# Gated cross-attention block: the next head group's scores ahead of this group's value products, and a second place for the exponentials

## The reference

```python
x = x + tanh(g_xattn[0]) * attention(layernorm(x), ctx, Wq, Wk, Wv, Wo)
# scores = Q K^T / sqrt(32); attn = softmax(scores) over 154 keys; out = (attn V) Wo^T
x = x + tanh(g_ffn[0]) * ffn(layernorm(x), W_r, W_k, W_v, mu_r, mu_k)
# x_prev = x shifted by one token
# xr = mu_r x + (1 - mu_r) x_prev, xk likewise with mu_k
# out = sigmoid(xr W_r^T) * (square(relu(xk W_k^T)) W_v^T)
```

## Time and profile before

| | |
|---|---|
| median of 3 runs | 1349.93 us |
| the profiled execution, whole | 1352.5 us |
| its span, first to last instruction | 1350.8 us |
| mean granted TensorE clock | 0.997 |
| TensorE busy with matmuls | 1324.2 us, 98% |
| TensorE weight loads | 992.8 us, 73% |
| VectorE | 1046.6 us, 77% |
| ScalarE | 778.0 us, 58% |
| GpSimd | 659.6 us, 49% |

### The profile page before, as it was taken

The page is one execution under the profiler, slowest core; times in us unless marked ns, Lnnn a source line. Parts: engine busy times, 40 slices in busy tenths (PEclk is TensorE's granted clock), DMA queues, the critical chain, the costliest instruction groups (busy, mean ns, idle before and its releaser), DMA issues.

```text
span 1350.8 us, 28900 instructions
## 1 busy us (share of the span) xinstructions
PE 1324.2 (98%) x9776; PEld 992.8 (73%) x9776; DVE 1046.6 (77%) x1983; ACT 778.0 (58%) x1457; POOL 659.6 (49%) x843
## 2 busy tenths in 40 slices
PE   6999999999999999999999999999999999999998
PEld 5667687777768677776877768777776877768777
DVE  6878778787886878778787887878788687877763
ACT  7655737466474655737466473745737465573633
POOL 7524445454444545445454445545445554444434
PEclk9998999999999999999999999999999999999999
DMA  9521312424123242312424222242413324231011
GB/s 311 155 59 48 91 51 78 116 55 128 44 84 77 62 132 54 99 45 77 112 54 132 59 77 66 62 132 54 122 33 85 93 54 139 54 92 48 32 48 40
DMA packets 160732, 113.27 MB, mean 84 GB/s; under 512 B 107456, under 2 KB 122304, under 8 KB 160704
## 3 DMA queue, kind: packets, MB, share of 16 engines
q1 hardware_dynamic: 160704, 112.91, 29.3%
HBM read 72.43 MB, written 35.39 MB: 80 GB/s over the span
## 4 chain that ended last, share of the span: by engine, by line
PE 88%; DVE 8%; ACT 3%; issue 1%; DMA 0%; DVEq 0%; ACTq 0%
PE g_bank L1415 41%; PE g_bank L1606 10%; PE o_bank L1546 7%; PE g_bank L1502 6%; PE s_bank L1520 4%; PE d_bank L1552 4%; PE s_bank L1530 3%; PE s_bank L1415 3%; PE s_bank L1478 3%; DVE buf L1006 2%; DVE o_bank L1194 2%; PE o_bank L1421 1%; DVE d_bank L1194 1%; PE s_bank L1524 1%; PE d_bank L1421 1%
## 5 line engine op out<-in xcount | busy, mean ns | idle before, releaser
L1099 DVE TENSOR_TENSOR pq<-s_bank,pq 128x512 f16<-128x512 f32 x320 | 220.0, 688 | 73.4 <-ACT s_bank L798 72.1
L1095 DVE TENSOR_REDUCE mm<-s_bank 128x3 f32<-128x462 f32 (+1 forms) x384 | 198.8, 578 | 74.6 <-PE s_bank L1478 74.6
L797 ACT ACTIVATE pq<-s_bank 128x512 f16<-128x512 f32 x320 | 194.3, 607 | 101.2 <-PE s_bank L1524 101.2
L798 ACT ACTIVATE s_bank<-s_bank 128x512 f32<-128x512 f32 x320 | 197.0, 616 | 0.0
L1606 PE MATMUL g_bank<-buf,WkT 128*128 128x512 f32 x720 | 189.7, 409 | 3.4 <-DVE buf L1006 3.3
L1415 PE MATMUL g_bank<-WrT,buf 128*128 128x512 f32 x744 | 183.7, 396 | 0.0
L1415 PE MATMUL g_bank<-WoT,buf 128*128 128x512 f32 (+1 forms) x768 | 175.4, 374 | 0.0
L1415 PE MATMUL g_bank<-WvT,buf 128*128 128x512 f32 x708 | 174.3, 395 | 0.0
L1415 PEld LDWEIGHTS g_bank<-WrT,buf 128*128 128x128 f32 x744 | 137.2, 188 | 39.3 <-issue 10.8
L1606 PEld LDWEIGHTS g_bank<-buf,WkT 128*128 128x128 f32 x720 | 131.4, 191 | 43.9 <-DVE buf L1006 9.6
L1415 PEld LDWEIGHTS g_bank<-WvT,buf 128*128 128x128 f32 x708 | 130.7, 188 | 32.4 <-issue 5.4
(11 more groups left out here) (186 smaller groups left out, 2304.6 us busy)
## 6 DMA issues: line engine op xcount, KB each, us to landing
xa<-in_x SPq DMA_DIRECT2D x64, 256.0 KB, 4.2
x<-in_x SPq DMA_DIRECT2D x64, 256.0 KB, 2.8
xt_scratch<-xa SPq DMA_DIRECT2D x28, 512.0 KB, 3.1
xnT_loaded<-xt_scratch SPq DMA_DIRECT2D x112, 128.0 KB, 3.2
out<-x SPq DMA_DIRECT2D x48, 256.0 KB, 2.3
place<-x SPq DMA_DIRECT2D x16, 256.0 KB, 2.4
out<-place SPq DMA_DIRECT2D x16, 256.0 KB, 2.0
k_all<-k_scratch SPq DMA_DIRECT2D x15, 256.0 KB, 3.3
```

Source lines behind the costliest of these rows:

```text
L797: nc.scalar.activation(pq[:, n, HI, :], bank[:, :], ACT.Exp, scale=SCALE).then_inc(p_hi, 1)
L798: nc.scalar.activation(bank[:, :], bank[:, :], ACT.Exp, scale=SCALE).then_inc(p_full, 1)
L1095: nc.vector.reduce_max(maxima, scores, AX.X).then_inc(reduced, 1)
L1099: nc.vector.tensor_tensor(pq[:, n, LO, :], score_bank[5 * g + n][:, :], pq[:, n, HI, :], ALU.subtract).then_inc(p_lo, 1)
```

## The change

TensorE's order in a step: `head_scores(i, g + 1)` moves ahead of `values(i, g)` for g = 0, 1, 2, in block 0 too. In loop steps (`ffn`) the tail scores of group g + 1 no longer stand between two products, but inside the first of them, behind its first three matmuls. The products keep their order.

In loop steps the exponentials of groups 0 and 2 get a place of their own, `p_even`, in the memory of `xnT`'s high part, and `p_even_tail`; groups 1 and 3 keep `pq`. ScalarE's wait before the exponentials of group g falls back by one group. Block 0 keeps one place and its old wait. On VectorE `attend(i, g - 1)` goes behind the first `p_low` of group g, and on ScalarE `attn_high(i, g - 1)` goes behind all five exponentials of group g, both in loop steps only. The array of maxima `mm` is packed from 512 to 140 columns. `xT_high_half` gets a wait for the values of group 2.

```diff
+        with nc.sbuf_tensor("p_even", [P, 4, 2, N], F16) as p_even:
+            pass
         xnT_loaded, xnT = parts("xnT")
...
+        p_even_tail = sb("p_even_tail", [P, 2, N], F16)
-        mm = sb("mm", [P, TT, P], F32)
+        mm = sb("mm", [P, P + 4 * (TT - 1)], F32)
...
+        def p_place(ffn, g, n):
+            if ffn and g % 2 == 0:
+                return p_even[:, n, :, :] if n < 4 else p_even_tail[:, :, :]
+            return pq[:, n, :, :]
...
             def xT_high_half(i, h, part):
                 act.wait_ge(xT_loaded[h], (i - 1) * 64)
+                act.wait_ge(av_done, i * G - 1)
...
-            def exps(i, g, n):
+            def exps(i, g, n, ffn):
...
-                later(act, av_done, i * G + g)
-                nc.scalar.activation(pq[:, n, HI, :], bank[:, :], ACT.Exp, scale=SCALE).then_inc(p_hi, 1)
+                later(act, av_done, i * G + g - 1 if ffn else i * G + g)
+                nc.scalar.activation(p_place(ffn, g, n)[:, HI, :], bank[:, :], ACT.Exp, scale=SCALE).then_inc(p_hi, 1)
...
-                    exps(i, g, 0)
-                    exps(i, g, 1)
-                    attn_high(i, g - 1)
+                    exps(i, g, 0, ffn)
+                    exps(i, g, 1, ffn)
+                    if not ffn:
+                        attn_high(i, g - 1)
...
-                    exps(i, g, 4)
+                    exps(i, g, 4, ffn)
+                    if ffn:
+                        attn_high(i, g - 1)
...
-                    attend(i, g - 1)
-                    p_low(i, g, 0)
-                    p_low(i, g, 1)
+                    if not ffn:
+                        attend(i, g - 1)
+                    p_low(i, g, 0, ffn)
+                    if ffn:
+                        attend(i, g - 1)
+                    p_low(i, g, 1, ffn)
...
+                head_scores(i, 1)
                 values(i, 0, not ffn)
 
-                head_scores(i, 1)
-                if ffn:
-                    ffn_r(i - 1, 1)
+                if ffn:
+                    ffn_r(i - 1, 1, at(1, lambda: tail_scores(i, 1)))
+                    ffn_v(i - 1, 0)
                 else:
                     keys_or_values(FIRST_LATER + 2)
-                tail_scores(i, 1)
-                if ffn:
-                    ffn_v(i - 1, 0)
-                else:
+                    tail_scores(i, 1)
                     keys_or_values(FIRST_LATER + 3)
+                head_scores(i, 2)
                 values(i, 1, not ffn)
```

More of the change, by code:

```diff
@@ L873, in step @@
                     xr_high(i - 1, 2)
-                exps(i, 0, 0)
-                exps(i, 0, 1)
+                exps(i, 0, 0, ffn)
+                exps(i, 0, 1, ffn)
                 if ffn:
@@ L878, in step @@
                     k2_high(i - 1, 1)
[L879 to L880 removed]
+                exps(i, 0, 2, ffn)
+                exps(i, 0, 3, ffn)
                 if not ffn:
                     kv_high(FIRST_LATER)
[L883 removed]
+                exps(i, 0, 4, ffn)
                 if ffn:
@@ L1092, in reduce_max, with p_low @@
                     scores = s_bank[j][:, 0:S * pairs].rearrange("p (n s) -> p n s", n=pairs)
-                    column = TAIL * j + g
-                    maxima = mm[:, t:t + pairs, column] if ROUNDS[r][-1][1] > t else mm[:, t, column:column + pairs]
+                    column, stride = TAIL * j + 4 * t + g, 4 if ROUNDS[r][-1][1] > t else 1
+                    maxima = mm[:, column:column + stride * (pairs - 1) + 1:stride]
                     nc.vector.reduce_max(maxima, scores, AX.X).then_inc(reduced, 1)
-            def p_low(i, g, n):
+            def p_low(i, g, n, ffn):
                 dve.wait_ge(p_full, i * SCORE_UNITS + 5 * g + n + 1)
-                nc.vector.tensor_tensor(pq[:, n, LO, :], score_bank[5 * g + n][:, :], pq[:, n, HI, :], ALU.subtract).then_inc(p_lo, 1)
+                place = p_place(ffn, g, n)
+                nc.vector.tensor_tensor(place[:, LO, :], score_bank[5 * g + n][:, :], place[:, HI, :], ALU.subtract).then_inc(p_lo, 1)
             def attend(i, g):
@@ L1246, in step @@
                     k_relu(i - 1, 2)
-                p_low(i, 0, 0)
+                p_low(i, 0, 0, ffn)
                 if ffn:
                     xr_low(i - 1, 3)
-                p_low(i, 0, 1)
-                p_low(i, 0, 2)
-                p_low(i, 0, 3)
+                p_low(i, 0, 1, ffn)
+                p_low(i, 0, 2, ffn)
+                p_low(i, 0, 3, ffn)
                 if not ffn:
                     kv_low_part(FIRST_LATER)
-                p_low(i, 0, 4)
+                p_low(i, 0, 4, ffn)
                 if ffn:
@@ L1273, in step @@
                         xT_low(i + 1, 0)
-                    p_low(i, g, 2)
-                    p_low(i, g, 3)
+                    p_low(i, g, 2, ffn)
+                    p_low(i, g, 3, ffn)
                     if not ffn and g < 3:
                         kv_low_part(FIRST_LATER + 2 * g)
-                    p_low(i, g, 4)
+                    p_low(i, g, 4, ffn)
                     if ffn:
@@ L1509, in maxima_transposed @@
                 later(pe, x2_ready, i * TT - 1)
-                transposed(mT_bank, [mm[:, t, :] for t in range(TT)]).then_inc(mT_done, 1)
+                transposed(mT_bank, [mm[:, 4 * t:4 * t + P] for t in range(TT)]).then_inc(mT_done, 1)
             def head_scores(i, g):
@@ L1545, in values @@
                             v = v_main[:, s, DH * (4 * g + j):DH * (4 * g + j + 1)] if n == 0 else v_tail[:, s, g, j, :]
-                            nc.tensor.matmul(o_bank[rows(j), :], v, pq[:, 4 if n else j, q, :],
+                            nc.tensor.matmul(o_bank[rows(j), :], v, p_place(not by_pe, g, 4 if n else j)[:, q, :],
                                              start=(n, k) == (0, 0), stop=(n, k) == (1, 2))
@@ L1551, in values @@
                             one = ones_main[:, :] if n == 0 else ones_tail[:, j, :]
-                            ins = nc.tensor.matmul(d_bank[rows(j), :], one, pq[:, 4 if n else j, q, :],
+                            ins = nc.tensor.matmul(d_bank[rows(j), :], one, p_place(not by_pe, g, 4 if n else j)[:, q, :],
                                                    start=(n, q) == (0, HI), stop=(n, q) == (1, LO))
@@ L1609, in ffn_k, with ffn_r @@
                             ins.then_inc(k_done, 1)
-            def ffn_r(i, t):
+            def ffn_r(i, t, beside=None):
                 if t < 2:
@@ L1617, in ffn_r @@
                 product(R_BANK[t][:, :], lambda s, c: buf2[:, s, c, cols(t)], lambda m, c: WrT[:, m, c, :], C,
-                        (lambda c: pe.wait_ge(xr_lo, i * C + c + 1)) if t == 0 else None).then_inc(r_done, 1)
+                        (lambda c: pe.wait_ge(xr_lo, i * C + c + 1)) if t == 0 else beside).then_inc(r_done, 1)
             def ffn_v(i, t, beside=None):
```

36 lines of the change are left out of this document (14 added, 22 removed).

## The result

| | before | after |
|---|---|---|
| median of 15 runs | 1353.11 us (1349.72 to 1355.21) | 1357.83 us (1356.27 to 1360.31) |
| profiled execution, whole | 1352.5 us | 1357.96 us |
| its span | 1350.78 us | 1356.24 us |
| mean granted clock of the span | 0.997 | 0.997 |

The changed kernel takes 1.0044 times as long, with a 95% interval of 1.0033 to 1.0054: slower by 4.5 to 7.3 us. The two profiled spans differ by 5.46 us. The forecast was +5.0 us, but from 1349.9, the median of the three runs then shown. With twelve more runs the median of before is 1353.11, so 1354.9 was forecast and 1357.83 measured.

The account below looks back on a forecast made before the run. TensorE, 98% busy, was taken to bound the kernel, losing nothing in the loop to the wait before the values. Loop 3.6, turns 0.3 and block 0 1.1 gave +5.0 us: median 1349.9 to 1354.9 us, range 1350.2 to 1358.8.

Parts of the forecast that it names:

- Carrying the sum to the median: Whole run: +5.0 us takes the profiled 1352.5 us to 1357.5, and the median from 1349.9 to 1354.9 us.
- The loop's new wait: Group 1's tail scores wait for the low part behind ScalarE's `k2_high` copy: 0.24 us per step, 15 steps, 3.6 us.
- The turns: Group 2's turns start 0.22 us later against TensorE, delaying the DRAM transfer before the query maxima: 0.3 us, bounds 0 to 3.1.
- Block 0: ScalarE waits at `attn_high` for the later `attend`, 0.54 us in groups 1 and 2: 1.1 us; group 3 zero.
- Boundaries: Loop steps: the new weight-shape boundary from scores to values costs the usual 0.10 us, zero net; ends -4.5 and +4.5 us.
- the thin cover of 0.3 us: Group 2's last low part ends at 638.67, the scores of group 3 want it at 639.03: zero cost.
- The real waits: Rival: TensorE's loop waits for the low parts before the values are real, giving 1342.4 us, faster; chance 0.07.
- Nothing in the loop: Rival: ScalarE's copy lets the exponentials go soon enough, so only block 0 costs, 1351.3 us; chance 0.18.
- free and double boundary: Rival: the scores-to-values boundary is free, 1350.4 us, chance 0.09, or costs double, 1359.4 us, chance 0.07.
- The clock: Rival: the clock drop around the end of block 0 is missed or comes longer, 1351.5 or 1358.3 us; chance 0.05.

Follow-up runs that it names:

- the last comparison: Changed kernel with three repairs (1351.97 us), and that with a second exponentials place in block 0 (1349.98 us), beside 23 runs of the kernel before (median 1352.65 us).
- Both cures: Changed kernel with group 1's tail scores behind six product matmuls, 1355.73 us; or with `k2_high(i-1, 3)` behind group 1's first pair of exponentials, 1355.75 us.
- the three positions of the tail scores: Group 1's tail scores behind zero, three (the changed kernel) or six product matmuls: 1368.50, 1357.83 and 1355.73 us.
- six profiled executions with these turns: Profiles of the changed kernel and five variants of it that leave the turns behind `attend`; query parts take 1.5 to 3.2 us beyond 5.46 per step.
- Turning earlier by 3.3 us: Changed kernel with the two turns of rows ahead of `attend` in group 2 of loop steps: 1356.69 us, ratio 1.0025.
- with `attend` behind: Changed kernel with, in block 0 alone, `attend` behind the first low part and `attn_high` behind the five exponentials: 1358.31 us in one run.
- all repairs: Changed kernel with group 1's tail scores behind six matmuls, turns ahead of `attend`, and block 0 in its old TensorE order: 1351.97 us, ratio 0.9991.
- one place: Changed kernel's order on all engines, but one place for all exponentials and their old wait: 1412.66 us in one run.
- tail scores alone: Kernel before with only the tail scores moved inside the products, behind three matmuls: 1415.42 us in one run.

## Why the prediction was right and wrong

- **Carrying the sum to the median: wrong, and the largest error.** "it is 2.6 above the median, so the median goes from 1349.9 to 1354.9 us." The sum was good: +5.0 forecast, +5.46 between the profiled spans, +4.7 between medians, +5.9 by the ratio. That is partly luck, since the loop was priced 0.8 us too high and the query part 1.2 too low. The step that failed is the base: it was a median of three runs, 1349.93 us, and fifteen give 1353.11. The profiled execution doesn't lie above the median of more runs; two of the three times shown, 1349.7 and 1349.9, lie where later runs lie that had almost no clock drop (the clocks of those three are not known). The 23 runs of the kernel before in the last comparison, by their mean clock: 1349.4 to 1350.7 us at 0.999 and 1.000 (seven), 1351.8 to 1351.9 at 0.998 (three), 1352.5 to 1353.6 at 0.997 (five), 1354.2 to 1356.3 at 0.996 and 0.995 (eight). The profiled one had 0.997, about the middle. From it the forecast would have been 1357.5, and 1357.83 was measured. In the earlier trace rows the drop shows, in the fourth slice (the prediction calls it the fifth); I used it for a rival and not for the base.
- **The loop's new wait: right in place and cause, somewhat smaller.** 0.14 of wait plus 0.10 of restart forecast, 0.09 plus 0.10 measured; 3.6 us became 2.8. The difference is in the second exponential (0.47 behind the first instead of 0.50), in VectorE's start, 0.03 behind ScalarE's end instead of 0.04, and in the copy, which starts 1.49 us ahead of the product instead of 1.47. Both cures remove it, and the three positions of the tail scores price it.
- **The turns: right mechanism, wrong size.** "in most steps it lands earlier. Bounds 0 and 14 x 0.22 = 3.1 us; I take 0.3." It is 1.5 us in the profile, and 1.5 to 3.2 in the six profiled executions with these turns. I had taken one step's landing as the latest and a shift of 0.22 us as the loss. The landings scatter by more than the shift, and in the one profiled execution of before, all 14 fell just inside the limit (latest 0.53 behind the query product, 0.5 allowed). Turning earlier by 3.3 us takes all of it away, so the chain is the cause. Why single landings came up to 0.8 us later than the latest of before, where the chain started only 0.24 later, stays open: in block 1 one load took 4.80 us, where the page's median from issue to landing is 3.1.
- **Block 0: right sum and right path, wrong about where it shows.** 1.1 forecast, 1.2 measured. In group 1 ScalarE's wait for `attend` costs 0.46 to 0.47 us (forecast: 0.54) and its later start 0.10; group 3, put at zero, takes 0.08. But I said that the waits in front of the scores would be about 0.5 us longer. They are at most 0.06 longer than those in front of the values were. TensorE stops at the tail scores of groups 1 and 2 instead, which start at 57.41 instead of 54.16 + 3.03 - 0.39 + 0.23 = 57.03 and then restart slowly, 0.48 us, and that shortens the wait behind it. The loop's order on the two engines doesn't mend it: with `attend` behind, 10.83 us of 10.91 remain, and VectorE is as late as ScalarE was.
- **Boundaries: zero, right.** 3.40 us in both orders, so the boundary from scores to values costs as the others. Groups 2 and 3 at 10.01 us: right, the thin cover of 0.3 us held (the last low part of group 2 ends at 641.36 + 0.67 = 642.03, the scores of group 3 start at 642.45).
- **The rivals.** The real waits (by the Trainium skill, Perfetto Trace Analysis, section Identifying the Most-Contended Engine, 27% of room): refuted, since VectorE's name is gone from those loads, their share is still 73%, and no time came back, not even with all repairs in (80.48 to 80.53 us a step against 80.50 to 80.53). Nothing in the loop, free and double boundary: refuted by 10.20 and by 3.40. The clock: it did fall at another place in the profiled execution, for 0.35 us net, an addition and not the decision; that the change moved it isn't shown.

## What to carry to other kernels

Before a wait is hidden, look at whether the engine's own starts show it: an idle weight load with a releaser's name beside it, and the same gap where nobody is waited for, is no wait. When an operation is moved up, check everything that stands ahead of its inputs on the other engines' queues; the copy ahead of the exponentials had been covered by a microsecond of idle time that the new order took away. Of two waits one behind the other, price the one that ends last: a stop ahead of it only shortens it. And ask of each base time in which clock it was taken, and of each transfer on the path how far its landing scatters, before pricing a shift of it.

## What the runs showed of the hardware

- A stop of 0.09 us in a stream of 512-column matmuls cost 0.19: the matmuls behind the wait pass 0.10 us later than in an unbroken stream (0.96 against 0.86 for three), whether TensorE waited 0.09 us, 0.22 (block 0), 1.02 (one place) or 1.38 (tail scores alone).
- The spread of one unchanged kernel, 1349.4 to 1356.3 us, goes almost wholly with the mean granted clock, 1.000 to 0.995. A drop of 3.4 us at half speed cost 1.7 us of matmuls (the values of group 3 in block 0, 3.95 us instead of 2.27) and is invisible in slices of 34 us.
- Transfers through DRAM that were started 14.45 us ahead of the query product, to within 0.01 us, in the 14 blocks of one execution, were ready for ScalarE over a range of 1.8 us.
